# A two-layer gated block on one core: an ACT step, a product, two gate steps and a load put at other places

## What is computed

```
x = x + tanh(g_xattn[0]) * _L0_xattn_ref(ctx_2048, ctx_2048, _layernorm(x), ssm_kernel, D, 8)
x = x + tanh(g_ffn[0])   * _L0_ffn_ref(_layernorm(x), base_W, router_W, A, B, biases)
x = x + tanh(g_xattn[1]) * _L1_xattn_ref(_layernorm(x), ctx_2048, wq, bq, wkv, bkv, wp, bp)
x = x + tanh(g_ffn[1])   * _L1_ffn_ref(_layernorm(x), gate, expert_bias, w1, w2, w3, shared_w1, shared_w2, shared_w3)
```

## Time and profile before

| what | us |
|---|---|
| median of 3 runs | 208.58 |
| lowest, highest run | 208.14, 209.37 |
| the profiled execution's own time | 209.84 |
| its span | 208.0 |
| PE busy (83% of the span) | 173.4 |
| DVE busy (79%) | 164.3 |
| ACT busy (51%) | 106.7 |
| POOL busy (41%) | 85.3 |

### The profile page before, as it was taken

The page is one execution under the profiler, slowest core; times in us unless marked ns, Lnnn a source line. Parts: engine busy times, 40 slices in busy tenths (PEclk is TensorE's granted clock), DMA queues, the critical chain, the costliest instruction groups (busy, mean ns, idle before and its releaser), DMA issues.

```text
span 208.0 us, 3594 instructions
## 1 busy us (share of the span) xinstructions
PE 173.4 (83%) x1156; PEld 110.6 (53%) x1156; DVE 164.3 (79%) x465; ACT 106.7 (51%) x280; POOL 85.3 (41%) x123
## 2 busy tenths in 40 slices
PE   0369999998998998978677968888789988998992
PEld 0226555557574555644245646655657735753660
DVE  0788989995347899997948999999994898577754
ACT  2450153201233243564158869889979885535540
POOL 1385566208295552167303220513222278409400
PEclk9999999999999999999658999999999999999998
DMA  5979962000000000000000000000000036936993
GB/s 170 393 225 367 392 241 80 0 3 0 0 0 2 0 3 2 0 0 0 2 3 0 0 5 0 3 2 3 0 3 0 3 74 130 129 76 113 187 206 101
DMA packets 22625, 15.17 MB, mean 73 GB/s; under 512 B 17648, under 2 KB 21328, under 8 KB 22096
## 3 DMA queue, kind: packets, MB, share of 16 engines
q1 hardware_dynamic: 21968, 13.94, 25.3%
q10 hardware_dynamic: 640, 1.02, 1.3%
HBM read 9.68 MB, written 1.07 MB: 52 GB/s over the span
## 4 chain that ended last, share of the span: by engine, by line
PE 42%; DVE 28%; issue 14%; DMA 6%; ACT 5%; POOL 4%; SPq 0%; DVEq 0%; POOLq 0%
PE PS L1334 5%; PE PS L1336 5%; PE PS L1335 5%; DMA X<-x 4%; PE PS L1422 4%; PE PS L1670 3%; DVE SM L1037 3%; PE PS L1398 3%; PE PS L1356 3%; DVE R L1047 3%; POOL R L507 2%; PE PS L1688 2%; PE PS L1365 2%; DVE T_R L975 2%; DMA R<-R 2%
## 5 line engine op out<-in xcount | busy, mean ns | idle before, releaser
L1037 DVE TENSOR_REDUCE SM<-PS 128x8 f32<-128x1024 f32 x16 | 18.8, 1212 | 3.7 <-PE PS L1498 2.5
L1512 PE MATMUL PS<-CON,R 128*128 128x128 f32 x128 | 19.0, 281 | 1.2 <-ACT R L669 1.2
L476 POOL TENSOR_TENSOR R<-R,CON 128x256 f32<-128x256 f32 x16 | 9.6, 618 | 25.3 <-PE PS L1498 16.2
L507 POOL TENSOR_SCALAR R<-QT,SM 128x256 bf16<-128x256 f32 x32 | 15.8, 511 | 9.9 <-DVE SM L1118 9.6
L341 POOL TENSOR_TENSOR R<-CT 128x512 f32<-128x512 f32 x12 | 13.4, 1113 | 13.6 <-PE PS L1336 7.8
L1277 DVE TENSOR_TENSOR R<-R,PS 128x512 bf16<-128x512 f32 (+1 forms) x17 | 11.6, 682 | 9.0 <-PE PS L1670 4.3
L669 ACT ACTIVATE R<-PS 128x512 f32<-128x512 f32 x32 | 18.4, 602 | 0.4 <-PE PS L1512 0.3
L1670 PE MATMUL PS<-R 128*128 128x512 bf16 x64 | 16.4, 379 | 1.2 <-DMA R<-R 1.2
L1512 PEld LDWEIGHTS PS<-CON,R 128*128 128x128 f32 x128 | 14.5, 143 | 3.7 <-issue 3.2
L567 ACT ACTIVATE LNV<-MV,EPSC 128x1 f32<-128x1 f32 (+1 forms) x22 | 6.5, 295 | 17.7 <-DVE MV L960 11.2
L1334 PE MATMUL PS<-R,T_R 128*128 128x384 f32 x32 | 13.8, 514 | 2.0 <-DVE T_R L852 2.0
(11 more groups left out here) (155 smaller groups left out, 431.1 us busy)
## 6 DMA issues: line engine op xcount, KB each, us to landing
WST<-w SPq DMA_DIRECT2D x3, 1024.0 KB, 11.2
T_R<-lagged SPq DMA_DIRECT2D x2, 768.0 KB, 7.6
X<-x SPq DMA_DIRECT2D x2, 512.0 KB, 6.8
CT<-ctxr SPq DMA_DIRECT2D x1, 1024.0 KB, 7.4
y<-X SPq DMA_DIRECT2D x8, 128.0 KB, 1.8
WKV<-wkv SPq DMA_DIRECT2D x1, 512.0 KB, 9.7
WQP<-wqp ACTq DMA_DIRECT2D x1, 512.0 KB, 6.2
R<-sw SPq DMA_DIRECT2D x3, 128.0 KB, 4.4
```

The source lines that it names most:

```text
L507: nc.gpsimd.tensor_scalar(XB[:, u % XS, j, :], MX[:, b, :], GG[:, b, e:e + 1], 1.0, ALU.mult, ALU.mult).then_inc(e_xb, 1)
L1037: V_.tensor_reduce(MX1[:, b % 2, 8 * c:8 * c + 8], S4[:, 8 * c:8 * c + 8, :], AX.X, ALU.max, negate=True).then_inc(a_mx, 1)
L1512: ins = TR(PS[:, 4 + k % 2, P * h:P * h + P], SS[:, b % 2, 4 * k + h, :], I)
```

## The change

It moves steps and adds none:

1. SP: the load of WKV goes behind the three `lags` loads.
2. DVE: `a_max(0, 0)` goes from the end of turn s = 8 of the second step's loop to the end of turn 9, where `a_max(0, 1)` is next.
3. PE: `a_scores(1)` goes ahead of `a_q_transpose(2)` in turn 0 of attention; ACT: `a_last_subtract(0)` goes ahead of `a_zt_(2)` and `a_q0_(2)` there.
4. ACT: `a_last_subtract(7)` goes behind `o_pe_(6)`, the copy of block 6's sums; `o_y_(4)` goes ahead of `m_rstd(3)`.
5. POOL: `expert_rows(3)` goes ahead of `late_rstd(5)`.
6. DVE: the product of unit 0 goes ahead of `finish(6)`, `m_stats(6)` and `third_rows(3)`.
7. DVE: the two parts of the second gates stand behind the products of units 5 and 6 (they stood behind 6 and 7), and ROWS_AT puts the rows of u = 8 into unit 6 on ACT and DVE.

```diff
-ROWS_AT = {1: (4,), 2: (5,), 3: (6,), 4: (7,), 7: (8, 9), 8: (10,), 9: (11, 12), 10: (13,), 11: (14,), 12: (15,)}
+ROWS_AT = {1: (4,), 2: (5,), 3: (6,), 4: (7,), 6: (8,), 7: (9,), 8: (10,), 9: (11, 12), 10: (13,), 11: (14,), 12: (15,)}
...
             lags(0, kern)
-            sp.dma_start(WKV[:, :, :], wkv).then_inc(L["wkv"], 16)
             sp.wait_ge(L["lag"], 16)
             lags(1, lagged)
             lags(2, lagged)
             lags(3, lagged)
+            sp.dma_start(WKV[:, :, :], wkv).then_inc(L["wkv"], 16)
...
             expert_rows(2)
+            expert_rows(3)
             late_rstd(GT + 1)
-            expert_rows(3)
             late_rstd(GT + 2)
...
             for s in range(NB):
+                if s == 0:
+                    a_last_subtract(0)
                 if s + 2 < NB:
                     a_zt_(s + 2)
...
-                a_last_subtract(s)
+                if 1 <= s < NB - 1:
+                    a_last_subtract(s)
...
+                if s >= 3:
+                    o_y_(s - 3)
                 if s == NB - 1:
                     m_rstd(NB - 5)
-                if s >= 3:
-                    o_y_(s - 3)
                 if s >= 1:
                     o_pe_(s - 1)
+                if s == NB - 1:
+                    a_last_subtract(s)
                 if s >= 5:
                     m_zt_(s - 5)
...
-                if s == NB:
+                if s == NB + 1:
                     a_max(0, 0)
...
-            finish(NB - 2)
-            m_stats(NB - 2, 0)
-            third_rows(3)
-            m_stats(NB - 2, 1)
...
                 V_.tensor_tensor(dst, HS[:, v % 2, :], PS[:, 3 + 2 * (v % 2), :], ALU.mult).then_inc(e_ht, 1)
                 if v == 0:
+                    finish(NB - 2)
+                    m_stats(NB - 2, 0)
+                    third_rows(3)
+                    m_stats(NB - 2, 1)
                     m_rows(NB - 3)
...
-                if v == GE_AT + 1:
+                if v == GE_AT:
                     for k in range(4):
                         m_gates(1, k)
-                if v == GE_AT + 2:
+                if v == GE_AT + 1:
                     for k in range(4, 6):
                         m_gates(1, k)
...
                     a_project(s + 2)
+                if s == 0:
+                    a_scores(1)
...
-                if s + 1 < NB:
+                if s >= 1 and s + 1 < NB:
                     a_scores(s + 1)
```

## The result

Over 20 executions each, taken in turn, the changed kernel took 209.6 us in the median (208.82 to 211.5) and the kernel before 208.69 (208.13 to 209.88). The ratio is 1.006, with a 95% interval of 1.004 to 1.008: slower by 0.8 to 1.7 us, where I had forecast no difference.

A forecast was written before the change was run, and what follows sets the result against it. PE (42% of the chain of waits) and DVE (28%) were taken to set the end. Terms -0.1 (load), +0.1 (entry), +0.3 (turn 7 through gates) gave +0.3 on the 208.58 us median: 208.9 us, range 207.3 to 209.9.

The forecast's parts named there:

- step 3: Entry to attention: block 1's scores start 1.0 us earlier, ACT's copies about 2 later with about that much room; +0.1.
- step 7: Second gates: the 0.89 us wait at unit 10 goes, silu 7 is held; unit 10 near 191.8 against 191.50.
- WKV, -0.1: Load at the start: X's second half arrives sooner, so DVE idles less; -0.1 us, between 0 and 0.27 to gain.
- steps 2 and 3: Entry to attention: DVE's subtractions of block 0 end some 0.55 us later, block 1's scores start 1.0 earlier; +0.1.
- The later clock: Rival at 110.6 us, entry to attention: the higher clock returns later; +1.5 us, 210.1 us, chance 0.15.
- ACT in turn 7, +0.8: Turn 7 of attention: moved subtractions delay `a_exp(7, 0)` by 0.9 us and what follows on PE by +0.8.
- The product, gives back 0.7: Unit 0: PE no longer waits for the product, giving back 0.7 of the 0.8 us; `e_out(0)` starts at 172.85.
- POOL, 0: POOL ahead of `late_rstd(5)`: `expert_rows(3)`, about 1.0 us, fits into 1.33 of idle time; effect 0.
- Gates, +0.44: Units 6 to 10: earlier gates hold silu 7, the unit 10 wait goes; unit 6 near 182.5, unit 10 near 191.8.
- The rival of the transposes: Units 5 to 8: POOL's rows come 0.7 us later, unit 6 starts at 183.3; +0.8, 209.4 us, chance 0.19.
- the entry's upper end: Entry to attention: upper bound of +0.55 us, if DVE's lateness went through.
- The gates': Upper bound at unit 10: +0.5 us, if `e_out(7)` were held for the full 1.4.

The follow-up runs named there:

- part 1 alone: The kernel before with only WKV's load moved behind the lags loads; 208.9 us, ratio 0.9987.

## Why the prediction was wrong

The sum was +0.3; the short groups and the medians say +0.9, the ratio +1.25 (0.6% of 208.6). By the traces the change is made up as follows; the profile of before is set against both profiles of the changed kernel, the entry against kernels with a like stretch of low clock:

| stretch | forecast | measured |
|---|---|---|
| load (part 1) | -0.1 | not told apart from 0 |
| entry to attention (parts 2 and 3) | +0.1 | about 0 (at block 3's transpose) to +0.5 (at block 2's maxima), by where the low clock begins |
| block 2's maxima to `m_ge_(0)` (part 4) | +0.8 | +0.68 |
| unit 0 to unit 6 (parts 5 and 6) | -0.94 | -0.81 to -0.82 |
| unit 6 to unit 10 (part 7) | +0.44 | +0.23 |
| unit 10 to unit 11 (part 7) | 0 | +0.41 |

Two steps failed: "they had about that much room" in step 3, at the entry, and "From unit 10 on the units follow each other at PE's pace as before" in step 7. Step by step:

- **WKV, -0.1**: not told apart from nothing. In the trace of part 1 alone the wait for X is 0.04 shorter, so the rule of ring order was the better guide.
- **The first maxima and the scores, steps 2 and 3, together +0.1.** DVE's lateness came as forecast, and the scores' start too. But part 2 is a gain, -0.6, and not a loss: I did not follow the earlier route through ACT and PE. And part 3 is +0.8 to +1.0 in its company. I wrote of ACT's copies that "they had about that much room": the one of block 3's rows came 2.28 us later relative to the first scores (I had said about 2) and the room was 1.7, so 0.64 arrived at block 3's transpose on PE. The wait was the right one and the room was mis-sized. The two errors have opposite signs; where together they come out near the +0.1, that is luck.
- **The later clock**, a rival at 0.15, came true in a third of the executions. "It decides where the clock is still 0.5 at 112" was the right place: 0.50 at 111 to 112 and at 113 to 114. The price of +1.5 was near (1.1 from one group to the next, 2.0 to 2.4 from short to long). But it is no either-or as I had it: it is a share of executions, which moves the median by part of its price. It is the smaller part of the loss here, since the short group is 0.9 slower too.
- **ACT in turn 7, +0.8**: right, +0.73 and +0.80 by time, +0.68 by trace, by the mechanism named. `a_exp(7, 0)` was to be 0.9 later and came 0.65 later behind the entry's loss; turn (7, 2) was to be 0.67 later, and was 0.54.
- **The product, gives back 0.7**: PE's wait is gone as said; by the units' distance -0.5, by time nothing alone and -0.8 beside part 2, which stays unexplained. I had seen that product 1 would be late; the 0.46 at unit 1 is that.
- **POOL, 0**: nothing seen against it; it was never run apart from the product.
- **Gates, +0.44 from unit 6 to unit 10 and nothing behind it.** Silu 7 held by the gates, `e_out(7)` late (1.12 of waiting by itself, "about 1.2" forecast) and the DMA wait gone at unit 10 all came as described, and up to unit 10 the loss was smaller than I said. What failed is the sentence "From unit 10 on the units follow each other at PE's pace as before". The 0.89 of waiting had covered DVE's product 9, rows and sums of group 0. Without it `e_out(9)` runs into them (0.15 to 0.44 of waiting in the rows) and unit 11 comes 3.01 us behind unit 10 for 2.60. So of the 1.12 late at `e_out(7)`, 0.89 is saved at unit 10 and 0.41 lost again: +0.64, which is what unit 6 to unit 11 shows. In the kernel before the same 1.72 of ACT's waiting for the gates held silu 8, whose output stands on PE behind the second shared unit's 3.60 us; one unit earlier nothing covers it.
- **The rival of the transposes** did not come true: unit 6 waited for none. One was late at unit 7 in the changed kernel (0.59) and in two others (0.53, 0.42); in the changed kernel the gates did not follow it.

The bounds: the entry's upper end was +0.55. The profiled execution had +0.79 there, but with 13.7 us of low clock for 10.2; with like stretches it is +0.5 at most, inside them. The gates' was +0.5, and they cost 0.64 to 0.66 once the way to unit 11 is counted.

Two slips in the rivals: the transposes' 209.4 and the later clock's 210.1 add their +0.8 and +1.5 to 208.6, though both come on top of the forecast of 208.9, so they should read 209.7 and 210.4. And the range has the centres of two rivals in it, not three.

## What to carry to other kernels

When a step moves ahead in one engine's list, ask not only who gets its result sooner: list what is queued behind it on its own engine, and which other engine waits for that. All three losses here are of this kind: the scores ahead of the q that ACT waits for, ACT's subtractions ahead of an exponential that PE waits for, ACT's rows of u = 8, themselves waiting, ahead of silu 7. So is the gain of part 2, where the maxima stood ahead of a route that PE's next steps waited for. Two moves can also undo each other: part 3 pays by how much earlier the scores start, and part 2 takes that away. A wait of PE for a DMA hides what else is due at that time, so before pricing its removal look up what the other engines end during it. And a bundle whose sum is near zero should be tried part by part: here parts 2, 5 and 6 make a kernel 0.65% faster, and the others turn that into 0.6% slower.
